# 256-row expert blocks with kept weights, token lists for rows, and the row quantiser beside the second attention's loop

## What is computed

```python
# layer 0
xn = layernorm(x)
x = x + attention0(xn) + moe(xn)
# layer 1
xn = layernorm(x)
x = x + attention1(xn) + (quantise(xn) @ quantise(w).T + bias)
```

## Time and profile before

| | us |
|---|---|
| median of 3 runs | 5565.52 |
| lowest and highest of them | 5412.44, 5870.92 |
| the profiled execution | 5408.28 |
| its span on core 5, first to last instruction | 5406.7 |
| spans of the other cores | 5362.9 to 5396.8 |

### The profile page before, as it was taken

One profiled execution on the slowest core, in us unless ns is written; L12 is line 12 of the kernel. 1 busy time (PEld: TensorE's weight loads), 2 busy tenths in 40 slices (PEclk: granted clock), 3 DMA queues, 4 the chain that ended last, 5 costly groups with the idle time before them and its releaser, 6 DMA issues.

```text
span 5406.7 us, 94922 instructions; the slowest of 8 cores (5362.9 to 5406.7 us)
## 1 busy us (share of the span) xinstructions
PE 4141.8 (77%) x37906; PEld 2068.6 (38%) x37906; DVE 1784.4 (33%) x3658; ACT 2444.4 (45%) x2679; POOL 282.1 (5%) x298
## 2 busy tenths in 40 slices
PE   1198898988985867689999991111699999899989
PEld 1043344433442323334444440000245554355554
DVE  2221112311122121211111116777455553355543
ACT  2137897378971101011211211111088892188881
POOL 0000100100000000000000002221100000000000
PEclk9998999989997878889999995555799999999999
DMA  4499833896025334355555545343310005300005
GB/s 137 131 237 129 130 52 107 163 125 106 2 70 185 144 142 161 126 194 213 196 219 214 195 171 183 140 148 109 69 26 10 6 33 149 66 10 10 6 18 156
DMA packets 270909, 633.66 MB, mean 117 GB/s; under 512 B 80288, under 2 KB 97552, under 8 KB 268048
## 3 DMA queue, kind: packets, MB, share of 16 engines
q1 hardware_dynamic: 146368, 351.49, 18.8%
q0 software_dynamic: 64800, 155.53, 16.8%
q10 hardware_dynamic: 59312, 120.59, 6.6%
HBM read 553.76 MB, written 233.83 MB: 146 GB/s over the span
## 4 chain that ended last, share of the span: by engine, by line
PE 60%; ACT 13%; DVE 11%; issue 7%; DMA 6%; ACTq 2%; DVEq 0%; SPq 0%; POOL 0%; POOLq 0%
PE m_py L1025 12%; ACT a_P L458 12%; PE m_ph L1004 12%; PE a_S L438 8%; PE a_acc L488 8%; PE a_F L328 6%; PE a_F L386 3%; PE a_acc L652 3%; PE a_F L652 3%; DMA m_fw<-l1fw 2%; ACTq L90 2%; PE a_S L450 1%; DVE n_xt L1136 1%; DMA n_xt<-x 1%; DMA a_QT<-x 1%
## 5 line engine op out<-in xcount | busy, mean ns | idle before, releaser
L458 ACT ACTIVATE a_P<-a_S 128x1024 bf16<-128x1024 f32 x2048 | 1954.2, 1053 | 565.6 <-PE a_S L438 382.2
L488 PE MATMUL a_acc<-a_V,a_P 128*128 128x65 bf16 (+1 forms) x16384 | 837.5, 197 | 66.1 <-issue 56.8
L1009 ACT ACTIVATE m_hT<-m_ph,m_b 128x512 bf16<-128x512 f32 x368 | 252.8, 687 | 1325.4 <-PE m_ph L1004 1325.4
L488 PEld LDWEIGHTS a_acc<-a_V,a_P 128*128 128x128 bf16 x16384 | 620.5, 99 | 425.5 <-issue 425.4
L438 PE MATMUL a_S<-a_QT,a_KT 64*128 64x512 bf16 (+2 forms) x3328 | 648.2, 381 | 117.2 <-ACT a_P L458 94.2
L1025 PE MATMUL m_py<-m_W,m_hT 128*128 128x512 bf16 x2944 | 653.2, 385 | 1.1 <-ACT m_hT L1009 1.1
L1004 PE MATMUL m_ph<-m_xT,m_W 128*128 128x512 bf16 x2944 | 641.3, 380 | 0.9 <-DVE m_xT L970 0.9
L1025 PEld LDWEIGHTS m_py<-m_W,m_hT 128*128 128x128 bf16 x2944 | 291.1, 99 | 354.0 <-issue 20.4
L1004 PEld LDWEIGHTS m_ph<-m_xT,m_W 128*128 128x128 bf16 x2944 | 288.4, 98 | 350.0 <-issue 4.0
L328 PE MATMUL a_F<-xn,a_wq 128*128 128x512 bf16 x1024 | 357.8, 392 | 2.6 <-issue 2.5
L328 PE MATMUL a_F<-xn,a_wk 128*128 128x512 bf16 x1024 | 353.5, 387 | 4.0 <-issue 4.0
(11 more groups left out here) (196 smaller groups left out, 3593.5 us busy)
## 6 DMA issues: line engine op xcount, KB each, us to landing
m_W<-W2b ACTq DMA_DIRECT2D x23, 4096.0 KB, 17.3
m_W<-W1b SPq DMA_DIRECT2D x23, 4096.0 KB, 14.3
Y<-m_ys SPq DMA_DIRECT2D x92, 512.0 KB, 3.2
W1b<-W POOLq DMA_DIRECT2D x8, 4096.0 KB, 43.8
W2b<-W POOLq DMA_DIRECT2D x8, 4096.0 KB, 74.6
a_QT<-x SPq DMA_DIRECT2D x64, 512.0 KB, 5.4
xg<-zt ACTq DMA_DIRECT2D x4, 5888.0 KB, 71.9
m_xs<-xg SPq DMA_DIRECT2D x23, 1024.0 KB, 16.5
```

The lines of the kernel that those rows point to most:

```text
L458: exps[i] = P.op("scalar", lambda e, s=s, i=i: e.activation(Pt[i % RING][:], s[:], AF.Exp, scale=scale), [tok, av_done.get(i - RING)], cha ...
L488: tok = P.op("tensor", lambda e, hh=hh, t=t, p=p, c=c, m=m: e.matmul(acc4[:, hh, t, 0:n_out(g, t, c)], p[:, 512 * hh + 128 * t:512 * hh + ...
L1009: ph_free[j % 2] = h_done[i] = P.op("scalar", lambda e, j=j, k=k: e.activation(hT[:, 512 * j:512 * (j + 1)], ph[j % 2][:], AF.Relu, bias=b ...
```

## The change

Layer norm: 12 buffers and loads three quads ahead; the statistics of quad q + 1 stand ahead of the normalising of quad q (`statistics(q + 1)`), on DVE and, for the root, on ACT. `emit_l1ln` has the same order, 12 buffers for tiles and 8 for each gather, no quantiser, no f32 copy and no cast on POOL.

Rows: `xg` and its zeros are gone. The routing also computes where in a list `slots` each token stands; 64 indirect scatters of token numbers fill it in the first attention (4 for each `side` call, the first 16 calls), and the expert stage gathers its rows from `xn0` through the list `tok`. Conversions come as 64 pieces (a quarter of one W1 or W2, 2 MB read and 1 MB written each), spread over 56 of the 64 `side` calls.

Experts: `BLK = 256`, `NBLK = 39`. Weights lie in one SBUF area `W` that the first attention uses for wq, wk, wv and wo; they come as 8 slices of 1 MB by indirect DMA from POOL. Where a block has the same expert as the one before it, the indices lie beyond the bound and the transfer leaves the old weights. The first W1 and half of W2 are loaded during the last pair of the first attention. Each up group is 8 matmuls of 256 columns; the down half runs over j outside and 4 PSUM banks inside. The weight quantiser's DVE work is issued in block i and its transposes (`turn_fd`) in block i + 1, with its input loaded one block ahead.

Second attention: the row quantiser is a generator advanced at steps where the masks are not near; q_x, q_u, q_p, q_d and q_t lie in `wbig` between its use for wv and for wo, and wo is loaded at step 474 of 512.

```diff
@@ emit_attention, rel=True
+            def quantise_rows(b, free_at):
+                for t in range(NT + 1):
+                    if t < NT:
+                        ld = P.dma("sync", q_x, x_in[b, 128 * t:128 * (t + 1), :], pre + "q_x", [x_done])
+                        yield
+                        xr = P.op("vector", lambda e, n=n: e.tensor_scalar(
+                            q_x, q_x, cfg["rs"][:, n:n + 1], cfg["nm"][:, n:n + 1],
+                            op0=ALU.mult, op1=ALU.add), [ld, free_at])
+                        yield
+                    if t:
+                        f = fb["n"] % 2
+                        for c in range(DC):
+                            tr = P.op("tensor", lambda e, c=c, f=f: e.transpose(...),
+                                [q_done, c_id, fb["free"][f]] if c == 0 else [], sig=(c == DC - 1))
+                        ev = fb["free"][f] = P.op("vector", lambda e, f=f: e.tensor_copy(
+                            q_t, F[f][:].bitcast(BF16)), [tr, sent], chain=False)
+                        sent = quantised[b] = P.dma("sync", cfg["xdT"][b, t - 1], q_t, pre + "q_t", [ev])
...
+                    for k, put in enumerate(puts):
+                        q_done = put()[-1]
...
+                        if k < len(puts) - 1:
+                            yield
...
-                    if c == 8:
+                    if not rel and c == 8:
                         next(side, None)
+                    if rel and c in (2, 4, 5, 7, 8, 10, 11, 13, 14) and not 4 * g - 1 <= c <= 4 * g + 4:
+                        next(side, None)
+                    if rel and (m, g, c) == (PAIRS - 1, 1, 10):
...
+                        wo_ld = P.dma("gpsimd", wbig3, wo3, pre + "wbig",
+                                      [P.now("pe"), P.now("dve"), quantised[b]])
@@ emit_l0att
-            keep["zeroed"].append(P.dma(
-                "scalar", xg3[:, lo:hi],
-                keep["zt"][:].unsqueeze(1).broadcast_to([128, hi - lo, D]), "n0_z%d" % i))
...
+        for y in range(PAIRS * GQ):
+            n = PAIRS * GQ * b + y
+            if n < 16:
+                for k in range(4):
+                    list_slots(P, io, keep, 4 * n + k)
...
+            for piece in range(64 * n // 56, 64 * (n + 1) // 56):
+                if piece < 64:
+                    narrow_weights(P, io, keep, piece)
+            yield
@@ emit_l0ln (and emit_l1ln)
+        ahead = statistics(0)
         for q in range(NTT // 4):
...
+            nrm = ahead
+            if q + 1 < NTT // 4:
+                ahead = statistics(q + 1)
@@ experts
-BLK = 512
+BLK = 256
...
+def load_slice(P, io, keep, name, i, k, after):
+    dst = keep["W"][:, 16384 * (name == "W2") + 4096 * k:16384 * (name == "W2") + 4096 * (k + 1)]
...
+        return e.indirect_dma_start(
+            dst, None, io[name + "b"], bass.IndirectOffsetOnAxis(
+                ap=keep["widx"][:, 4 * i + k:4 * i + k + 1], axis=0),
+            bounds_check=keep["bound"], oob_is_err=False)
...
+                    tok_pe = P.op("tensor", lambda e, j=j, c=c, k=k: e.matmul(
+                        ph[j % 2][:, 0:BLK], ...
+                        xT[k][:, BLK * c:BLK * (c + 1)], start=(c == 0), stop=(c == DC - 1)),
+                        [w_ld[("W1", i, j // 4)], xT_done[i], ph_free[j % 2]] if c == 0 else [],
...
+                if more and j % 4 == 3:
+                    load_slice(P, io, keep, "W1", i + 1, j // 4, tok_pe)
+            xT_read[i] = tok_pe
+            if more:
+                load_bias(i + 1)
+                turn_x(i + 1)
+            if 0 < i <= DC:
+                turn_fd(i - 1)
+            if i < DC:
+                quantise(i)
...
+                if more and j % 4 == 3:
+                    load_slice(P, io, keep, "W2", i + 1, j // 4, tok_pe)
```

More of the change, by code:

```diff
@@ L199, in emit_attention @@
             tvwo = Pt[4][:]
+            q_x, q_u, q_p = [wbig[:, 2048 * i:2048 * (i + 1)].bitcast(F32) for i in range(3)]
+            q_d, q_t = wbig[:, 6144:7168], wbig[:, 7168:8192]
+            q_am, q_sc, q_rc = cfg["small"]
             E3 = [t[:].rearrange("p (h k) -> p h k", h=2) for t in E]
@@ L743, in emit_l0ln, with fetch, statistics @@
         xb_read = [None] * 4
+        xt_read, lds = {}, {}
+        def fetch(q):
+            for n in range(4 * q, 4 * q + 4):
+                lds[n] = P.dma("sync", xt[n % 12][:], x0[n // NT, 128 * (n % NT):128 * (n % NT + 1), :],
+                               "n0_xt%d" % (n % 12), [xt_read.get(n - 12)])
+        def statistics(q):
+            o = 48 * (q % 2)
+            for k in range(4):
+                n = 4 * q + k
+                for h in range(2):
+                    P.op("vector", lambda e, k=k, h=h, n=n: e.bn_stats(
+                        st[:, o + 12 * k + 6 * h:o + 12 * k + 6 * h + 6],
+                        xt[n % 12][:, 512 * h:512 * h + 512]), [lds[n]], chain=False)
+            P.wait("vector", P.now("dve"))
+            for k in range(4):
+                agg = P.op("vector", lambda e, k=k: e.bn_aggr(
+                    mv3[:, 4 * q + k], st[:, o + 12 * k:o + 12 * k + 12]), chain=False)
+            four = slice(4 * q, 4 * q + 4)
+            sq = P.op("scalar", lambda e: e.activation(
+                sd[:, four], mv3[:, four, 1:2].squeeze(2), AF.Sqrt, bias=eps[:, 0:1]),
+                [agg, e_set], chain=False)
+            P.op("vector", lambda e: e.reciprocal(rs[:, four], sd[:, four]), [sq])
+            return P.op("vector", lambda e: e.scalar_tensor_tensor(
+                nm[:, four], mv3[:, four, 0:1].squeeze(2), -1.0, rs[:, four],
+                op0=ALU.mult, op1=ALU.mult))
+        for q in range(3):
+            fetch(q)
+        ahead = statistics(0)
         for q in range(NTT // 4):
@@ L864, in emit_l0ln @@
+        V(lambda e: e.tensor_scalar(keep["ids"][:], seq[:, 0:NTT], 128.0, row,
+                                    op0=ALU.mult, op1=ALU.add))
+        bl = sm[:, 192:192 + 7 * NBLK].rearrange("p (i e) -> p i e", e=7)
+        tt(bl, seq.unsqueeze(2).broadcast_to([128, NBLK, 7]),
            sa[:, 1:8].unsqueeze(1).broadcast_to([128, NBLK, 7]), ALU.is_ge)
-        ef = sm[:, 320:320 + NBLK]
+        ef, off, old = [sm[:, 480 + 40 * i:480 + 40 * i + NBLK] for i in range(3)]
         red(ef, bl, ALU.add)
-        off = sm[:, 384:384 + NBLK]
@@ new lines, in emit_l0ln, with list_slots @@
+        V(lambda e: e.tensor_scalar(off, off, 4.0, None, op0=ALU.mult))
+        V(lambda e: e.scalar_tensor_tensor(off, old, 2.0 * WROWS, off, op0=ALU.mult, op1=ALU.add))
+        wx = keep["widx"][:].rearrange("p (i k) -> p i k", k=4)
+        for k in range(4):
+            keep["routed"] = V(lambda e, k=k: e.tensor_scalar(
+                wx[:, :, k:k + 1].squeeze(2), off, float(k), None, op0=ALU.add))
+def list_slots(P, io, keep, n):
+    keep["listed"].append(P.put_dma("gpsimd", lambda e: e.indirect_dma_start(
+        io["slots"], bass.IndirectOffsetOnAxis(ap=keep["sl"][:, n:n + 1], axis=0),
+        keep["ids"][:, n % NTT:n % NTT + 1], None), "ls%d" % (n % 4),
+        [keep["blank"], keep["routed"]]))
@@ L983, in quantise, with turn_fd @@
+        def turn_fd(r):
             for c in range(DC):
@@ new lines, in emit_l1ln @@
+                for c in range(DC):
+                    tr = P.op("tensor", lambda e, c=c, k=k: e.transpose(
+                        pT[k][:, 128 * c:128 * (c + 1)], xb[k][:, 128 * c:128 * (c + 1)], idb[:]),
+                        [xn, c_id, pt_free[k]] if c == 0 else [], sig=(c == DC - 1))
+                xb_read[k] = tr
+            for k in range(4):
+                tr = xb_read[k]
+                ev = pt_free[k] = P.op("scalar", lambda e, k=k, dst=dst: e.copy(
+                    dst[:, :, 128 * k:128 * (k + 1)],
+                    pT[k][:].rearrange("p (c t) -> p c t", t=128)),
+                    [tr, P.now("n1_xT%d" % g)], chain=False)
```

526 lines of the change are left out of this document (255 added, 271 removed).

## The result

| | before | after |
|---|---|---|
| median of 4 runs on one chip, us | 5492.69 | 4947.84 |
| lowest and highest | 5412.44, 5870.92 | 4809.01, 5047.02 |
| ratio after / before, 95% interval | | 0.893 (0.872 to 0.914) |

Faster, as forecast, but 277 us later than the 4671 of the forecast and outside its range. In part of the executions one die runs at a lower clock whatever the kernel; the medians hold such executions, and the ratio leaves them out (of six of the changed kernel it uses 4809.01 and 4862.39). In the lowest run, 4809.01, cores 0 to 3 take 4767 to 4807 us and cores 4 to 7 take 4697 to 4715. So two things are to be explained: why a core without trouble takes 4707 us where 4670 were forecast, and why four of the cores take up to 100 more.

The account below looks back on a forecast made before the run. Each stage has its own limit, such as PE in the experts and DVE in the second layer norm. Terms -413 - 29 - 45 - 17 - 20 - 293 + 80 = -737 took 5406.7 to 4671 us; range 4530 to 4890.

Parts of the forecast that it names:

- Experts, -413: Expert stage: 39 blocks of 28.7 us plus small extras, 1143 us against 1556, with weight transfers and the weight quantiser hidden.
- rival 5: Expert weights: indirect transfers cost POOL their time whether they move or not; break-even 5.3 us a slice; 5619 us, 1%.
- rival 4: Experts: beyond-bound transfers move the old expert's weights anyway, 36 us a block, +280, 4950 us; chance 4%.
- Second attention, +80: Second attention's two loops: the row quantiser on DVE overfills a pair of heads, 73.8 us against 70.4; +80 (38 to 162).
- I take 40: Second attention: chosen loss of 40 us a sequence, between 19 from DVE's sum and 81 if waits before masks are lost.
- Rival 3: Second attention: DVE bounds the loop, every quantiser operation delays it in full, 333 us instead of 80; 4924 us, 7%.
- First attention, -20: First attention's loops: 34 MB of scatter traffic go, so conversions cost 124 us instead of 145.
- rivals 1 and 2: Conversions spread over both first-attention loops either slow every step (4812 us, 13%) or disturb nothing (4546 us, 12%).
- rival 2: First attention: the spread conversions disturb nothing in the loops, 4546 us; chance 12%.
- Second layer norm, -293: Second layer norm: transfers bound it, 71.3 MB at 300 GB/s plus 35 us for first landing and tail, 273 against 566.
- First layer norm with routing: First layer norm: load wait and some chain gaps go, 162 us against 211; routing adds 4; term -45.
- Start of the first attention: First attention's start waits for wv, which lands in 17.5 us without the zeros instead of 34.8; -17.

Follow-up runs that it names:

- the spread kernel: The changed kernel with the second attention's row quantiser at 18 slots a pair of heads instead of 23; loops 593 to 604 us, a pair 76 us instead of 82.4.

## Why the prediction missed

**Experts, -413.** Right in its parts where nothing disturbs: 1145 us against 1143, a block of 29.0 against 28.7, and in the timeline of core 5, against the earlier trace rows:

```profile
2240.54 14.22 PE L1095 MATMUL m_ph<-m_xT,W 128*128 128x256 bf16 x128
...
2255.70 14.03 PE L1122 MATMUL m_py<-W,m_hT 128*128 128x512 bf16 x64
```

The blocks came as summed, and the weight quantiser vanished from PE's waits. The slices are issued in 1.0 us each, far below the 5.3 of rival 5; kept blocks move no weights (rival 4 fell). The step that failed on four of the cores is a term that was put at nothing: for the ReLU the working counted 0.31 us of signal and the length of the operation, always, and it let core 5 stand for all cores. A group of 0.86 us on two banks has no room for a late signal. The prediction costed the gathers of rows in POOL's time and held that nothing but transfers stands behind them. On one die the gathers make PE's signals 1 to 3 us late in 37 of 39 blocks, which is 92 us over the stage on core 1 (70 of waits, 22 of longer matmuls). The trace of before could not show it: there the experts' rows were loaded plainly, and the loads lay in the middle of the block.

**Second attention, +80.** The mechanism was right and the size was off: the failed step is "I take 40", between the 19 and the 81 a sequence of its two bounds. Measured are 76. DVE's work and gaps come to 71.5 us a pair (73.8 forecast), and the waits in front of the masked probabilities and of `acc`, 11 us, stay in full, so the upper bound was the right one. The middle had no reason. The rule behind it (DVE is full when work reaches the pair's length) is refuted by the spread kernel, which has room by that rule (59.4 + 6 of 69.5) and still pays 6.5 us a pair. Rival 3, every operation in full, would have been 333 us.

**First attention, -20.** It came to -14. The number is nearly right, and part of that is luck. The sum counted bytes, and bytes explain it only because the traffic is as bunched as before. The statement that it is spread thinly over all steps was wrong, and rivals 1 and 2 were built on it: neither could come true while POOL's queue ran ahead by itself. Made true by a wait, rival 2 is what happens on core 5 (12 us lost instead of 124). The reading that PE's idle stretches without a releaser are fetches of its instructions was right.

**Second layer norm, -293.** Bytes right (230 us at 315 GB/s are 72.5 MB, forecast 71.3), the rate 315 instead of 300, and the 35 us for the first landing and the tail were hardly there: 71.3 MB at 315 are 226 of the 230 us. The DMA engines are busy from the start to some 17 us before the end, share 0.94, so this transfer-bound stage needed almost no margin at its ends.

**The small terms.** First layer norm with routing -50.5 (-45): 162 us as forecast, and the routing's new operations disappeared. Start of the first attention -14.5 (-17), of the experts -23 (-29).

**The sum.** Core 5: 4670 + 72.5 - 44.5 + 9.5 = 4707. That it lies within 37 us is in part luck, since two errors of 72 and 44 us have opposite signs. The slowest core has 92 more in the experts and some from the first loop, 4807. Up to there the range held. The median of the runs lies 139 above the lowest run, 2.9%, the same excess that the prediction read from the runs before; it gave 4807 only because the forecast under it was 138 too low.

## What to carry to other kernels

Ask of every transfer on a queue what holds it back: a queue that waits for nothing runs ahead, and its traffic is bunched however its instructions are spread in the code. Tying it to the loop that it should accompany brought 112 us in the loops of an undisturbed core, 71 on the slowest, for one wait.

When a loop's groups get shorter, count how late a signal may be before the engine stops, and put indirect transfers where the busiest engine waits for nobody. And read the slowest core of the changed kernel by itself: that all cores were alike before does not carry over. For work put beside a loop, the other engine's waits for its own inputs are not room; take them as lost.

## What the runs showed of the hardware

- Behind two indirect gathers of 128 rows of 2 KB, PE's semaphore signals can come 1 to 3 us late, on the cores of one die and not of the other: mostly 51 to 86 late ReLUs of 624 on each of the four, 0 to 10 on the others. Landing signals of transfers go on arriving meanwhile. Plain loads of the same size leave 0 to 5. On that die the attention's exponentials stand for up to 3.2 us behind indirect scatters that run beside conversions.
- An indirect transfer whose indices are all beyond the bound costs POOL its 1.0 us, and no delay was seen from it.
- Conversions from HBM to HBM, with the scatters, make a step of the loop 1.23 us (315 us for 256) instead of 0.93 at a DMA share of 1.0, and 0.95 at a share of 0.5. At the share of 1.0 PE stands at 13 of its 22 instruction fetches, for up to 4.8 us.
- A POOL operation of 2.3 us over SBUF makes DVE's bf16 masks 32 to 36% longer in the mean.
